# Splitting the second half of the key and query weights inside groups 0 and 1

## Chip, cores and metric

The kernel runs on one core of a Trainium2 chip. Its time is the device time of one execution in microseconds (us). The times before are 2044.08, 2043.05 and 2043.65 us, median 2043.65.

## What is computed

An input of 16 sequences of 512 tokens with 128 features goes through a layer norm; to the input are added an attention over the normed rows and a mixture of experts over them. All is in float32. Cut to what matters:

```python
xn = layernorm(x)
# attention: 16 heads of 64
h = rmsnorm(xn) * norm_scale
q, k, v = h @ wq, h @ wk, h @ wv          # each 128 x 1024
a = softmax((q * 64 ** -0.5) @ k.T) @ v   # per head
attn = a @ w_out + b_out
# experts: 8, the two best of each token
logits = silu(xn @ rw1 + rb1) @ rw2 + rb2
w, i = top_k(logits, 2); w = softmax(w)
ffn = sum(w_e * (silu(xn @ w1[e] + b1[e]) @ w2[e] + b2[e]))
out = x + attn + ffn
```

## The kernel before

Matrix products with the weights are done with each operand split into a high part (rounded to the faster float32r type) and a low part (the rest), as three matmuls into one PSUM bank (`three`, lines 237 to 240: low times high, high times low, high times high). The weights are split once. `split_weights` does this for chunks of 512 columns: ACT writes the high part (line 245), then either DVE (line 248) or POOL (line 252) subtracts it from the source and writes the low part. The raw weights are staged in parts of PT, a tile that later holds transposed probabilities.

Chunk 0 of WK and WQ serves head pairs 0 to 3 of a batch element, chunk 1 pairs 4 to 7. A pair of heads is worked on in two groups, so chunk 1 is first needed by the projections for pair 4.

The program is a list of operations for each engine, filled by `add` and emitted in order. Each operation has a name and the names that it needs, which become semaphore waits. Operations added between two calls of `q.close()` are sorted within an engine by their place: for DVE in a group with an even number the order is inverse, max0, max1, turn1, turn0, low, values, sums, side; in an odd one sums, max0, turn0, max1, turn1, values, inverse, low, side. For ACT it is turn0, exp00, exp01, high, exp10, exp11, values, side, hi, turn1 in an even group and turn0, exp00, values, exp01, high, turn1, exp10, side, exp11, hi in an odd one. What has no place goes to "side", in the order in which it was added. PE, POOL and SP keep the order of the program.

In front of the groups (the head of the program) stand: the statistics and normed rows of batch element 0, the split of chunk 0 of WK and WQ, the transposes into HT, the projections of pair 0 (`project`, whose result is split by ACT on line 378 and DVE on line 379), then a block of remaining splits (lines 866 to 870), the small operation RB1H (line 871, 4 columns on DVE), a memset of PM (872), and `turn_x(0)`, the transposes into XT with a cast on ACT (343) and the low part on DVE (344).

Then come groups 0 to 261, `group(G)`. On PE an even group runs scores S0, transposes T0, scores S1, T1, the next projection (kq), attending, experts and routing. Scores are line 394, row maxima of them DVE line 403, exponentials ACT line 409 with an accumulator read, transposes of probabilities PE line 424, copied out by ACT line 436 or DVE line 439. In group 0, `attending` adds four value tiles (lines 238 to 240 on PE; copied out by DVE on line 361 for the first, ACT on line 359 for the others), and `route` adds the first router matmuls (L238 to L240 with R), followed on ACT by TANH (line 555) and the copy HS (558), on POOL by lines 561 and 563. Reciprocals of the row sums are line 464. `starting(G)` is called inside the experts part of each group, before `route`, and adds what is to be done once at that group.

A planner (`take`, with fixed costs in `HOLD`) chooses PSUM banks while the program is written. The order of its choices isn't changed by operations that take no bank. Its choice for the third value tile of group 0 is the bank that held the key projection of pair 1, free once DVE has written that one's low part.

Of the kernel before, what the change touches and what calls it, by code (L numbers as in the profile page):

```python
# [20 lines left out]
DH = 64  # L21
# [44 lines left out]
class Queues:  # L66
# [7 lines left out]
    def add(self, engine, make, needs=(), name=None, step=1, sem=None, place="side"):  # L74
        key = None
        if name is not None:
            key = sem or (engine + "_" + name[0])
            self.count.setdefault(key, 0)
        self.open[engine].append((place, make, [n for n in needs if n is not None], name, key, step))
# [23 lines left out]
def block_kernel(nc, x, wq, wk, wv, wout, ns, bout, rw1, rb1, rw2, rb2, w1, w2, bias, ident, tri, consts, out):  # L103
# [11 lines left out]
    with ExitStack() as ctx:  # L115
        def sb(name, shape, dt=F32, to=ctx):
            return to.enter_context(nc.sbuf_tensor(name, shape, dt))
# [7 lines left out]
        WQ = sb("WQ", [P, 2, H * DH], F32R)  # L125
        WK = sb("WK", [P, 2, H * DH], F32R)
# [105 lines left out]
        wk_s = PT[:, 2, 0:2].rearrange("p a b -> p (a b)")  # L232
        wq_s = PT[:, 2, 2:4].rearrange("p a b -> p (a b)")
# [8 lines left out]
        def split_weights(name, src, dst, chunks, scale=1.0, on="pool"):  # L242
            for c in chunks:
                s = slice(c * 512, (c + 1) * 512)
                add("act", lambda e, s=s: e.mul(dst[:, 0, s], src[:, s], scale), needs=[("load", f"{name}{c}")],
                    name=("whi", name, c))
                if on == "dve":
                    add("dve", lambda e, s=s: e.scalar_tensor_tensor(dst[:, 1, s], src[:, s], scale, dst[:, 0, s],
                                                                     ALU.mult, ALU.subtract),
                        needs=[("whi", name, c)], name=("wlo", name, c))  # L250
                else:
                    add("pool", lambda e, s=s: e.tensor_tensor(dst[:, 1, s], src[:, s], dst[:, 0, s], ALU.subtract),
                        needs=[("whi", name, c)], name=("wlo", name, c))
# [610 lines left out]
            project(0, key)  # L864
        q.close()
        split_weights("wv", wv_s, WV, [0])
        split_weights("wk", wk_s, WK, [1], on="dve")
        split_weights("wv", wv_s, WV, [1])
        split_weights("wq", wq_s, WQ, [1], DH ** -0.5, on="dve")
        split_weights("r1", r1_s, R1, [0])  # L870
        add("dve", lambda e: e.tensor_scalar(RB1H[:], RB1[:], 0.5, None, ALU.mult), needs=[("load", "rb1")], name=("rb1h",))
        add("dve", lambda e: e.memset(PM[:, 0, 0], 0.0), name=("pm0",))
# [4 lines left out]
        turn_x(0)  # L877

        def starting(G):
            if G == 10:  # L880
                add("pool", lambda e: e.tensor_scalar(BIN[:, :, 8:16], BIN[:, :, 0:8], 0.5, None, ALU.mult),
                    needs=[("load", "bias")], name=("bhalf",))
            if G == 11:
                add("sp", lambda e: e.dma_start(b_tab.rearrange("e p c -> p e c"), BIN[:]), needs=[("bhalf",), ("load", "bias")],
                    name=("b_tab",), step=16, sem="b_tab")
            if G == 13:
                add("sp", lambda e: e.dma_start(out[T:T + S].rearrange("(t p) d -> p t d", p=P), PAD[:, :, 0:D]),
                    needs=[("pad0",)], name=("spare_out",), step=16, sem="spare_out")
            if 14 <= G < 14 + E - 1:
                k = G - 14  # L890
                add("sp", lambda e: e.dma_start(slots[E * REGION + k * S:E * REGION + (k + 1) * S]
                                                .rearrange("(t p) d -> p t d", p=P), PAD[:]),
                    needs=[("pad",)], name=("pads", "x", k), step=16, sem="pads")
            if G == 22:
                add("sp", lambda e: e.dma_start(out[EARLY * S:T], x[EARLY * S:T]), name=("base",), step=16, sem="base")
# [126 lines left out]
        def group(G):  # L1022
# [13 lines left out]
            for part in PE_ORDER[odd]:  # L1036
                if part in ("S0", "S1"):
                    score(int(part[1]))
                elif part in ("T0", "T1"):
                    if old:  # L1040
                        turn_probs(*old[int(part[1])])
                elif part == "kq":
                    if live and n + 1 < PAIRS:
                        project(n + 1, odd == 0)
                elif part == "inverse":
                    if even:
                        denominators(G // 2 - 1)
                elif part == "ahead":
                    halves_after(G)
                elif part == "attend":  # L1050
                    attending(G)
                elif part == "spread":
                    if even:
                        spread(G // 2 - 1)
                elif part == "route":
                    route(G)
                elif part == "experts":
                    starting(G)
                    splitting(G)
                    counting(G)  # L1060
                    experts(G)
                    again(G)
                elif part == "weighted":
                    if odd and 0 <= G - 3 < GROUPS:
                        weighted((G - 3) // 2)
# [76 lines left out]
```

How the kernel before makes its waits and increments, by code:

```python
    def emit(self, engine, eng, sems):  # L91
        seen = {}
        for make, needs, key, step in self.items[engine]:
            for sem, value in (self.value[n] for n in needs):
                if seen.get(sem, 0) < value:
                    eng.wait_ge(sems[sem], value)
                    seen[sem] = value
            ins = make(eng)
            if key is not None:
                ins.then_inc(sems[key], step)
# [974 lines left out]
        @block.sync  # L1075
        def _(eng):
            q.emit("sp", eng, sems)
            for k, v in q.count.items():
                if k.startswith(("st_", "sadd", "spare_out", "base", "rrow", "tab", "b_tab", "sc_", "pads")):
                    eng.wait_ge(sems[k], v)
```

## Time and profile before

| | |
|---|---|
| runs | 2044.08, 2043.05, 2043.65 us |
| profiled execution | 2040.24 us, span 2038.4 us |
| PE busy | 1947.9 us, 96% |
| ACT, DVE, POOL busy | 77%, 76%, 45% |
| mean granted TensorE clock | 0.99 |

A granted clock of 1.00 is 2.4 GHz and one of 0.50 is 1.2 GHz. Times of instructions are counted from the start of the span. Records of one engine may overlap by about 0.1 us, since an engine starts an instruction while the last one drains: the step from one start to the next is then less than the duration.

### The profile page before, as it was taken

The numbers are of one execution on the slowest core, as the hardware profiler recorded it, in microseconds if no ns is written. First come the engines' busy times: TensorE is split into PE (matmuls) and PEld (weight loads), VectorE is DVE, ScalarE is ACT, GpSimd is POOL, SyncE is SP. The second block draws the span as 40 slices with busy tenths as digits, with TensorE's granted clock in tenths as the row PEclk, the third lists the DMA queues.
The fourth block names the chain that finished last, engine by engine and source line by source line (L and its number), as shares of the span: only waits on it lengthen the run. The fifth ranks groups of instructions, "written<-read, shape, count | busy, mean of one in ns | idle before, by whom it ended". The sixth has DMA issues, their size and how long they took to land.

```text
span 2038.4 us, 45230 instructions
## 1 busy us (share of the span) xinstructions
PE 1947.9 (96%) x16646; PEld 1254.4 (62%) x16646; DVE 1539.4 (76%) x2654; ACT 1574.2 (77%) x3716; POOL 918.2 (45%) x790
## 2 busy tenths in 40 slices
PE   7999999999999999998889999999999999999997
PEld 5655555555656555564556666666666666666664
DVE  6878888887878777776767777777777777777774
ACT  5777777777777777775678888888888888888884
POOL 4344455453344444441014645546446455464454
PEclk9999999999999999999999999999999999999999
DMA  2023222221111111001313334344333343343332
GB/s 84 30 61 103 91 98 89 85 72 34 40 37 43 38 43 38 33 32 36 91 57 81 84 86 84 80 95 85 85 79 85 86 83 88 84 85 80 79 75 47
DMA packets 132697, 141.96 MB, mean 70 GB/s; under 512 B 25438, under 2 KB 99038, under 8 KB 132446
## 3 DMA queue, kind: packets, MB, share of 16 engines
q1 hardware_dynamic: 101886, 118.34, 18.4%
q0 software_dynamic: 30592, 20.73, 8.6%
q8 instruction: 134, 2.20, 0.5%
q14 instruction: 85, 0.70, 0.1%
HBM read 102.65 MB, written 38.46 MB: 69 GB/s over the span
## 4 chain that ended last, share of the span: by engine, by line
PE 75%; ACT 12%; DVE 6%; issue 4%; DMA 2%; another core or an unknown queue 1%; SPq 0%; POOL 0%; POOLq 0%; DVEq 0%; ACTq 0%
PE pair L453 21%; PE pair L394 15%; PE pair L424 10%; PE pair L238 6%; PE pair L240 5%; PE pair L239 4%; ACT PR L409 4%; PE pair L499 2%; PE pair L501 2%; DVE NM L403 2%; PE pair L787 1%; PE pair L788 1%; PE pair L786 1%; ACT PT L436 1%; ACT HS L558 1%
## 5 line engine op out<-in xcount | busy, mean ns | idle before, releaser
L409 ACT ACTIVATE PR<-pair,NM 128x512 f32<-128x512 f32 x1024 | 718.2, 722 | 21.3 <-DVE NM L403 18.8
L403 DVE TENSOR_REDUCE NM<-pair 128x2 f32<-128x1024 f32 x512 | 611.8, 1211 | 68.0 <-PE pair L394 47.9
L436 ACT COPY PT<-pair 128x512 f32<-128x512 f32 x640 | 358.2, 608 | 368.4 <-PE pair L424 364.4
L394 PE MATMUL pair<-KS,QS 64*128 64x512 f32 x3072 | 491.7, 424 | 20.5 <-DVE KS L379 12.3
L453 PE MATMUL pair<-PT,V 128*64 128x512 f32 x2048 | 471.0, 602 | 0.2
L424 PEld LDWEIGHTS pair<-idn,PR 64*128 64x128 f32 x8192 | 338.0, 139 | 100.8 <-ACT HS L558 27.0
L394 PEld LDWEIGHTS pair<-KS,QS 64*128 64x128 f32 x3072 | 257.8, 188 | 181.1 <-issue 126.2
L424 PE MATMUL pair<-idn,PR 64*128 64x64 f32 x8192 | 343.2, 223 | 21.0 <-ACT HS L558 15.9
L813 POOL DMA_INDIRECT out<-YS,IDW x156 | 246.9, 1583 | 187.2 <-DVE YS L805 128.6
L778 POOL TENSOR_TENSOR HH<-ZZ,HH 128x512 fp32r<-128x512 f32 x156 | 199.2, 1347 | 291.1 <-ACT HH L775 291.1
L453 PEld LDWEIGHTS pair<-PT,V 128*64 128x64 f32 x2048 | 136.4, 137 | 258.7 <-issue 252.5
L439 DVE COPY PT<-pair 128x512 f32<-128x512 f32 x384 | 250.8, 681 | 14.7 <-remote 9.6
L409 ACT ACTIVATION_READ_ACCUMULATOR PR<-pair,NM 128x1 f32 x1024 | 242.1, 236 | 0.0
L561 POOL TENSOR_TENSOR TH<-TH,HS 128x512 f32<-128x512 f32 x64 | 81.8, 1278 | 295.9 <-ACT HS L558 295.6
L459 DVE TENSOR_TENSOR OT<-pair,RB 128x512 f32<-128x512 f32 x128 | 88.4, 690 | 144.8 <-PE pair L453 136.2
L772 DVE SCALAR_TENSOR_TENSOR ZZ<-ZT,ZZ 128x512 f32<-128x512 f32 x156 | 110.5, 709 | 79.2 <-ACT ZZ L763 79.1
L664 POOL DMA_INDIRECT slots<-XR,IDX x128 | 125.8, 983 | 89.9 <-DVE junk L660 58.8
L379 DVE TENSOR_TENSOR QS<-pair,QS 128x512 fp32r<-128x512 f32 x128 | 88.5, 691 | 90.0 <-ACT QS L378 87.7
L761 ACT ACTIVATE ZT<-pair,BT 128x512 f32<-128x512 f32 x156 | 116.6, 747 | 1.5 <-PE pair L240 1.4
L763 ACT ACTIVATE ZZ<-pair,BT 128x512 f32<-128x512 f32 x156 | 117.7, 754 | 0.0
L379 DVE TENSOR_TENSOR KS<-pair,KS 128x512 fp32r<-128x512 f32 x128 | 87.3, 682 | 9.3 <-ACT KS L378 9.1
L378 ACT CAST QS<-pair 128x512 fp32r<-128x512 f32 x128 | 77.9, 609 | 15.6 <-PE pair L240 9.3
(168 smaller groups left out, 2807.9 us busy)
## 6 DMA issues: line engine op xcount, KB each, us to landing
E<-w_tab SPq DMA_DIRECT2D x78, 512.0 KB
RB<-l_rows SPq DMA_DIRECT2D x127, 256.0 KB
XG<-slots SPq DMA_DIRECT2D x39, 264.0 KB
w_tab<-SPL SPq DMA_DIRECT2D x16, 512.0 KB
l_rows<-RT SPq DMA_DIRECT2D x508, 1.0 KB
xin<-in_x SPq DMA_DIRECT2D x16, 256.0 KB
XQ<-in_x SPq DMA_DIRECT2D x16, 256.0 KB
RAW<-in_w SPq DMA_DIRECT2D x16, 256.0 KB
```

The costliest lines, as they stand in the source:

```text
L238: e.matmul(ps, w[1], m[0], start=True, stop=False)
L379: add("dve", lambda e: e.tensor_tensor(lo, bank[bk], hi, ALU.subtract), needs=[(name + "hi", n), *old], name=(name + "lo", n), place="low")
L394: m = e.matmul(bank[bk + j], a[half[j], cols], c[half[j], :], start=(k == 0), stop=(k == 2))
L403: add("dve", lambda e: e.tensor_reduce(NM[:, 2 * t:2 * t + 2], both[:], AX.X, ALU.max, negate=True), needs=[("S", n, t), *([("exp", n - 1, ...
L409: add("act", lambda e: e.activation(PR[:, k, :], bank[bk], ACT.Exp, bias=NM[:, k:k + 1], accum_out=RS[:, n % 2, j, t:t + 1]), needs=[("max ...
L424: m = e.transpose(bank[two[r]][:, at:at + DH], PR[rows, 2 * t + j, c * P:(c + 1) * P], idn[rows, rows])
L436: add("act", lambda e, r=r: e.copy(dst[r], src[r]), needs=[("T", n, t), *old], name=("PT", n, t, r), place=f"turn{t % 2}")
L439: add("dve", lambda e, r=r: e.tensor_copy(dst[r], src[r]), needs=[("T", n, t), *old], name=("PT", n, t, r), place=f"turn{t % 2}")
L453: m = e.matmul(bank[bk][j * DH:(j + 1) * DH, :], V[:, k, h * DH:(h + 1) * DH], PT[:, n % 2 * 2 + j, k, :], start=(k == 0), stop=(k == QT - 1))
L664: add("pool", lambda e, k=k, t=t: e.indirect_dma_start(slots, bass.IndirectOffsetOnAxis(ap=IDX[:, r % 2, k, t:t + 1], axis=0), XR[:, r % 2 ...
L778: add("pool", lambda e: e.tensor_tensor(lo, ZZ[:, r], hi, ALU.subtract), needs=[("hi", n), old], name=("lo", n))
L813: add("pool", lambda e, t=t: e.indirect_dma_start(out, bass.IndirectOffsetOnAxis(ap=IDW[:, i % 4, t, 0:1].bitcast(U32), axis=0), YS[:, i % ...
```

## The change

Two of the seven calls of `split_weights` are taken out of the head and done by `starting` in groups 0 and 1. Each is one operation on ACT and one on DVE, with 128 x 512 elements each. By the sorting rule they come to stand in "side": the one of WK behind the value copies of group 0 and in front of the router's TANH on ACT, and last in group 0 on DVE; the one of WQ between the last two exponentials of group 1 on ACT, and last in group 1 on DVE. No transfer is moved.

```diff
         split_weights("wv", wv_s, WV, [0])
-        split_weights("wk", wk_s, WK, [1], on="dve")
         split_weights("wv", wv_s, WV, [1])
-        split_weights("wq", wq_s, WQ, [1], DH ** -0.5, on="dve")
         split_weights("r1", r1_s, R1, [0])
...
         def starting(G):
+            if G == 0:
+                split_weights("wk", wk_s, WK, [1], on="dve")
+            if G == 1:
+                split_weights("wq", wq_s, WQ, [1], DH ** -0.5, on="dve")
             if G == 10:
```

## Rows read from the trace of the kernel before

**Rows 1.** The page: its span, and the busy time of each engine.

```profile
span 2038.4 us, 45230 instructions
...
PE 1947.9 (96%) x16646; PEld 1254.4 (62%) x16646; DVE 1539.4 (76%) x2654; ACT 1574.2 (77%) x3716; POOL 918.2 (45%) x790
```

**Rows 2.** Windows: us, busy PE, PEld, DVE, ACT, POOL, granted clock, DMA, GB/s.

```profile
17.30:21.30 4.00, 3.95 (x21) 2.66 (x21) 3.68 (x3) 2.33 (x5) 4.00 (x3) 1.00 0.00 0
21.30:26.30 5.00, 0.00 (x0) 0.00 (x0) 4.14 (x7) 2.67 (x8) 1.29 (x4) 0.99 0.00 0
26.30:30.20 3.90, 3.87 (x10) 3.12 (x11) 0.57 (x1) 2.24 (x5) 0.00 (x0) 0.57 0.00 0
...
36.20:40.00 3.80, 3.79 (x36) 3.07 (x38) 1.59 (x4) 2.51 (x7) 0.66 (x1) 0.55 0.01 1
```

**Rows 3.** Chain that ended last, in order of time: start us, us, what.

```profile
15.46 0.23 PE pair L239
...
17.07 0.53 ACT WK L245
...
17.62 1.37 DVE WK L248
19.00 1.70 DVE WQ L248
20.70 1.64 DVE RB1H L871
...
22.39 1.22 DVE NM L403
...
27.55 0.43 PE pair L240
```

**Rows 4.** Line 248: duration in ns, least/median/most, first and last start in us.

```profile
L248 DVE SCALAR_TENSOR_TENSOR WK<-PT,WK x2: 693/1033/1373, 7.0 to 17.6; 128x512 fp32r<-128x512 f32 x2
L248 DVE SCALAR_TENSOR_TENSOR WQ<-PT,WQ x2: 679/1228/1777, 11.8 to 18.9; 128x512 fp32r<-128x512 f32 x2
```

**Rows 5.** Timeline of DVE: start us, us, instruction, idle before and its releaser.

```profile
16.57 0.69 DVE L379 TENSOR_TENSOR QS<-pair,QS 128x512 fp32r<-128x512 f32 x1
...
21.79 0.67 DVE L344 TENSOR_TENSOR XT<-pair,XT 128x512 fp32r<-128x512 f32 x1
...
31.82 2.48 DVE L403 TENSOR_REDUCE NM<-pair 128x2 f32<-128x1024 f32 x2 [4.95 <-PE pair L394]
...
37.36 0.20 DVE L464 RECIPROCAL RI<-RS 128x8 f32<-128x8 f32 x1 [1.20 <-ACT PR L409]
...
37.73 1.20 DVE L403 TENSOR_REDUCE NM<-pair 128x2 f32<-128x1024 f32 x1
```

**Rows 6.** Timeline of ACT.

```profile
19.05 0.57 ACT L343 CAST XT<-pair 128x512 fp32r<-128x512 f32 x1
...
29.29 0.59 ACT L359 COPY V<-pair 128x512 f32<-128x512 f32 x1 [0.69 <-PE pair L240]
30.23 0.69 ACT L555 ACTIVATE TH<-pair,RB1H 128x512 f32<-128x512 f32 x1 [0.35 <-PE pair L240]
...
36.41 0.76 ACT L409 ACTIVATE PR<-pair,NM 128x512 f32<-128x512 f32 x1
...
38.56 1.07 ACT L436 COPY PT<-pair 128x512 f32<-128x512 f32 x2 [1.29 <-PE pair L424]
```

**Rows 7.** Timeline of POOL.

```profile
17.16 2.99 POOL L252 TENSOR_TENSOR WV<-PT,WV 128x512 fp32r<-128x512 f32 x2 [5.38 <-ACT WV L245]
20.11 1.73 POOL L252 TENSOR_TENSOR R<-PT,R 128x512 fp32r<-128x512 f32 x1
```

**Rows 8.** Timeline of PE, the restarts after standing still.

```profile
14.27 0.50 PE L238 MATMUL pair<-HT,WK 128*128 128x512 f32 x1 [1.63 <-DVE HT L329]
...
26.33 0.80 PE L238 MATMUL pair<-WV,HT 128*128 128x512 f32 x1 [5.05 <-DVE KS L379]
...
36.21 1.46 PE L394 MATMUL pair<-KS,QS 64*128 64x512 f32 x6 [1.79 <-DVE QS L379]
```

## Prediction

> **What bounds the kernel now.** I read the page first. PE is busy for 1947.9 us of a 2038.4 us span [rows 1], so most of the kernel is PE's, and a change that moves four small instructions can only be worth something where PE stands still. The second view is the table of windows over the first 40 us, because the four instructions stand there [rows 2]. From 17.3 to 21.3 us PE is busy 3.95 of 4.00 us; from 21.3 to 26.3 us it does nothing at all, while DVE is busy 4.14 us; from 26.3 to 30.2 us it is busy again, with ten matmuls in 3.87 us and a granted clock of 0.57 (a mixture of the two levels, 1.2 and 2.4 GHz, mostly the lower); from 36.2 to 40.0 us the clock is low again, 0.55.
>
> The third view is the chain of work that ended last, in order of time [rows 3]. The reader is to see that it walks through the very instructions of the change: the high half of WK's second chunk on ACT (0.53 us), then on DVE its low half (1.37 us), WQ's low half (1.70 us) and the small RB1H operation (1.64 us), and only then the first row maxima, at 22.39 us. Behind those maxima come the exponentials, the cast of the next key tile, its low half on DVE, and that last one frees PSUM bank 0, for which PE has waited 5.05 us when it starts the third value tile at 26.33 us [rows 8]. So the start of the program is one serial chain, and DVE's queue is its longest link. Nothing after it follows the clock on the wall: each later stage is released by instructions of the one before, and the four moved instructions take no PSUM bank, so the written order of all else stays as it is.
>
> **Step 1: what the removal in front of group 0 gives.** After the low half of Q (16.57 us, 0.69 long, to 17.26) DVE's queue will hold RB1H, then XT's low half, PM's memset, and the first maxima [rows 5]. Two things can hold it. XT's low half needs ACT's cast of XT, which began at 19.05 us [rows 6]; two ACT instructions of 0.53 us each [rows 3] leave the queue in front of it, so it begins at 19.05 - 1.06 = 17.99, ends 0.57 later at 18.56, and DVE can start on it at about 18.6. RB1H is the other. It has four columns, and took 1.64 us of the chain. The same low halves that took 0.69 and 0.68 us at the very start took 1.37 and 1.78 us here [rows 4], and what is different is that POOL runs its own subtractions, two in 2.99 us from 17.16 and a third of 1.73 us from 20.11 [rows 7]: XT's low half starts at 21.79, just as that third one ends (20.11 + 1.73 = 21.84). I read this as DVE and POOL taking turns. In the new order RB1H comes at 17.3, inside POOL's first subtraction, which ends half way through the 2.99 us, at about 18.65. That is the time at which XT's cast is ready too, so RB1H costs nothing beyond it. From XT's low half to the maxima it was 22.39 - 21.79 = 0.60 us. The maxima start at 18.6 + 0.6 = 19.2 in place of 22.39: **3.2 us** gained. The first scores are there in time: PE starts them when Q's low half is done at 17.3, and the 21 matmuls up to 21.3 are the 12 of the scores and nine dense ones behind them at 0.23 us [rows 2, 3], so the scores end at about 19.
> The bounds: if RB1H gets its turn only when POOL's second subtraction ends (17.16 + 2.99 = 20.15), the maxima start at 20.75 and 1.6 us are gained. More than 3.2 is excluded by XT's cast. The Trainium skill (GPSIMD Engine Reference, section 8, Key points) says that GpSimd shares its SBUF interfaces with VectorE and contends with instructions of two SBUF inputs or of a 2-port mode, and says nothing of turns: by it alone RB1H could be held for as long as POOL's subtractions follow each other, which would make step 1's term the 1.6 us or less and not the 3.2.
>
> **Step 2: PE's clock behind the stall.** The stall shrinks from 5.05 to 5.05 - 3.2 = 1.85 us. After the 5.05 us stall the clock was at the low level, and a dense matmul took a step of 0.43 us where it takes 0.23 at the high one [rows 3]. Is 1.85 us short enough to keep 2.4 GHz? The rows point both ways: before the first projection PE stood still for 1.63 us and the window behind shows no fall; before the scores at 36.21 it stood still for 1.79 us, and those six took 1.46 us at the low level [rows 8, 2]. What differs is the work around: in front of the second were transposes of 64 columns, in front of the first and of ours dense matmuls of 512. I take it that the clock holds, with the other case as a rival.
> Its worth is read at the next place where the chain is on ACT, the first TANH of the router at 30.23 us, 3.90 us after PE's restart [rows 6, 8]. At the high level the two value tiles take 0.4 us for the last matmul, 5 steps of 0.23 and some 0.1 for the first, 1.65 us; then ACT copies the last of them (one step of 0.53), does the moved high half of WK (0.53, see below) and reaches TANH 2.75 us after the restart, when PE's nine matmuls (2.35 us) are done as well. 3.90 - 2.75 = 1.15, and I take **1.2 us**. If the clock falls as before, this term is gone and turns into a cost of 0.1: the value copy starts 29.29, and two steps of 0.53 end at 30.35 in place of 30.23.
>
> **Step 3: what is added in group 0.** ACT's part is counted above. DVE's low half of WK (0.69 us alone; POOL has nothing to do at that time, its next work waits for the router) falls into the 4.95 us for which DVE waits in front of the next group's maxima [rows 5]: nothing. Without that cover it would be 0.7 us.
>
> **Step 4: what is added in group 1.** ACT's high half of WQ goes in front of the group's last exponential, which began at 36.41 us; behind it ACT waited 1.29 us for PE's transposes [rows 6], so 0.53 us are covered. DVE's low half of WQ (0.68 us) falls into the 1.20 us of waiting in front of the reciprocal; the reciprocal moves by 0.53 us, and the maxima behind it from 37.73 to about 38.2, ending 1.20 later at 39.4 [rows 5]. What needs them is an exponential that stands behind two copies on ACT which end at 38.56 + 1.07 = 39.63 and pass the engine on about 0.1 earlier [rows 6]. Covered, by a tenth of a us. If it isn't, or POOL doubles the operation to 1.78 us [rows 4], it costs 0.1 to 1.0 us. The queues of SP and POOL lose and get nothing: the first transposed probabilities that overwrite the staged weights are written at the earliest in group 3, two groups behind the last moved split, so their wait on it is met long before.
>
> **Sum.** 3.2 + 1.2 = 4.4 us, against the profiled execution's 2040.24 us (span 2038.4), which makes 2035.8. The median of the runs is 2043.65, 3.4 above that execution, and the change takes the same off it: 2043.65 - 4.4 = **2039.2 us**. 0.2% of the median is 4.1 us, about what a measurement of this kernel can tell from no change; the forecast lies just beyond it.
>
> **The rivals.**
> (a) The clock falls behind the short stall too. Rows 8 show it once after 1.79 us of standing still. Then the gain is 3.2 - 0.1 = 3.1: 2040.6 us. The Trainium skill (TensorE: Matmul & The Clock Gate, Part 1, What's actually happening) says that the clock's switching point isn't tied to the kernel's start and differs from run to run. No run here shows that; by it, several executions of one program would differ in this term, which the three times (1.0 us apart) neither show nor exclude. I give it 2 in 10.
> (b) RB1H waits for a second subtraction: the lower bound of step 1. Gain 1.6, with the clock's 1.2 at most 2.8: 2040.9 to 2042.0 us. Against it: between POOL's back-to-back subtractions WK's low half did get its turn (it ended at 18.99, 0.35 us after the first of them). 1 in 10.
> (c) The gain is given back later: the chain behind 40 us is bound elsewhere, or the moved instructions displace what is critical in group 1. Gain 0 to 1.5: 2042.2 to 2043.7. Against it: everything is released by this chain. 0.6 in 10.
> (d) Slower: PE's clock falls at other places. A fall costs about what it cost here, 1.2 us; the earlier start moves the work against the moments at which it switches, and later stages have stalls of PE of over a us too. It takes four more falls than now to use up 4.4 us, and eight to make the kernel slower by 0.2%; six would give 2043.65 - 4.4 + 7.2 = 2046.5 us. 0.4 in 10.
> (e) The forecast, 2039.2 us: 6 in 10. Its own range is 2038.3 to 2039.9: another 0.5 us if the second fall, at 36 us, goes away as well, 0.7 less if step 4's thin cover fails.
>
> **How the numbers follow.** The range reaches over the forecast, (a) and half of (b): 2038.3 to 2041.2, about 8 in 10. Faster by over 0.2% (below 2039.56) is three quarters of (e), with a little of the rest: 0.46. Slower by over 0.2% is the far part of (d): 0.03. The rest, 0.51, is within 0.2%, as a smaller gain, though the likeliest single time lies just outside.
>
> **What would show it.** In the profile after: the first row maxima at about 19.2 us, RB1H and XT's low half in front of them; PE's stall behind the second value tile about 1.9 us, with value matmuls of 0.4 us and not 0.63; the first TANH near 25.8 us; low halves of WK and WQ of about 0.7 us each, in DVE's waits near 26 and 32.7; PE's busy share unchanged. The prediction is wrong if the maxima start later than 20 us (step 1), if the granted clock behind the stall is 0.5 (step 2), or if the head shows the 4.4 us and the end doesn't.

## The result and the profile after

Over 17 runs of each, the changed kernel takes 2038.91 us (median) and the kernel before 2043.26 us. The ratio is 0.9979, with a 95% interval from 0.9972 to 0.9987: faster by 4.4 us, and by something between 2.7 and 5.7. The forecast was a gain of 4.4 us. (The three runs in front of the prediction had a median of 2043.65 us, the 17 one of 2043.26.)

The profiled execution of the changed kernel took 2040.83 us and that of before 2040.24, so these two executions show no gain at the end, although one is there at the head. Both halves of that have to be read.

The head first. Timeline of DVE in the changed kernel (start us, us, instruction, idle before), the counterpart of [rows 5] and [rows 3]:

```profile
15.82 0.69 DVE L379 TENSOR_TENSOR KS<-pair,KS 128x512 fp32r<-128x512 f32 x1 [1.68 <-ACT KS L378]
...
17.13 1.30 DVE L869 TENSOR_SCALAR RB1H<-RB 128x4 f32<-128x4 f32 x1
...
18.57 0.69 DVE L344 TENSOR_TENSOR XT<-pair,XT 128x512 fp32r<-128x512 f32 x1
19.18 2.35 DVE L403 TENSOR_REDUCE NM<-pair 128x2 f32<-128x1024 f32 x2
...
26.40 0.69 DVE L248 SCALAR_TENSOR_TENSOR WK<-PT,WK 128x512 fp32r<-128x512 f32 x1 [2.72 <-ACT WK L245]
...
33.79 0.69 DVE L248 SCALAR_TENSOR_TENSOR WQ<-PT,WQ 128x512 fp32r<-128x512 f32 x1 [1.00 <-ACT WQ L245]
```

The first row maxima start at 19.18 us in place of 22.39 [rows 3]. The moved low halves take 0.69 us each where they took 1.37 and 1.78 [rows 4], and stand in waits. RB1H waits for POOL's first subtraction and no longer sets anything: XT's low half follows ACT's cast.

PE's restart and the clock, timeline and windows of the changed kernel, the counterpart of [rows 8] and [rows 2]:

```profile
23.13 0.50 PE L238 MATMUL pair<-WV,HT 128*128 128x512 f32 x1 [1.93 <-DVE KS L379]
23.47 0.39 PE L239 MATMUL pair<-WV,HT 128*128 128x512 f32 x1
...
24.16 0.63 PE L239 MATMUL pair<-WV,HT 128*128 128x512 f32 x1
...
32.85 0.96 PE L394 MATMUL pair<-KS,QS 64*128 64x512 f32 x6 [1.59 <-DVE QS L379]
...
21.30:23.10 1.80, 0.00 (x0) 0.00 (x0) 0.94 (x3) 1.80 (x6) 0.36 (x3) 1.00 0.00 0
23.10:27.40 4.30, 4.27 (x12) 3.16 (x12) 1.27 (x2) 3.59 (x8) 0.00 (x0) 0.62 0.00 0
27.40:34.50 7.10, 5.31 (x70) 3.90 (x69) 4.43 (x5) 6.96 (x17) 5.08 (x4) 0.98 0.01 2
34.50:37.90 3.40, 3.33 (x24) 2.82 (x25) 3.16 (x5) 2.37 (x6) 0.00 (x0) 0.52 0.01 1
```

The stall is 1.93 us in place of 5.05. But the clock still fell: the matmuls are 0.39 us long at first and 0.63, the length at 1.2 GHz, from 24.1 us on. It fell again at 34.4 us. On ACT:

```profile
25.73 0.63 ACT L245 ACTIVATE WK<-PT 128x512 fp32r<-128x512 f32 x1
26.53 0.69 ACT L555 ACTIVATE TH<-pair,RB1H 128x512 f32<-128x512 f32 x1 [0.17 <-PE pair L240]
...
33.08 0.67 ACT L245 ACTIVATE WQ<-PT 128x512 fp32r<-128x512 f32 x1
33.60 0.73 ACT L409 ACTIVATE PR<-pair,NM 128x512 f32<-128x512 f32 x1
...
36.10 0.69 ACT L409 ACTIVATE PR<-pair,NM 128x512 f32<-128x512 f32 x1 [0.68 <-DVE NM L403]
```

The first TANH comes at 26.53 us in place of 30.23 [rows 6], 3.7 us earlier. PE's first scores of group 1, which follow at 27.66 us in place of 30.81, are only 3.15 us earlier. The last row is a wait that the kernel before does not have in this place, 0.68 us behind the row maxima of group 2, to which the split of WQ has made DVE late.

At the first attention output (line 459, pair 0) the changed kernel is 3.0 us ahead: 47.99 against 51.01. It is still 3.0 ahead at the seventh output, 131.16 against 134.13. At the 61st, 912.51 against 912.17, nothing is left of it. Whether the change or the execution took that back was the first question.

### The profile page after: what moved, and what is told of

Its sections match the earlier page's. It is cut to its first block, busy times and chain, and to the rows that moved or that the text cites. A ratio compares the mean times of both kernels' runs of the same rounds, so it can differ in the third digit from the quotient of the medians.

```text
span 2039.0 us, 45230 instructions
## 1 busy us (share of the span) xinstructions
PE 1950.4 (96%) x16646; PEld 1257.1 (62%) x16646; DVE 1538.8 (75%) x2654; ACT 1576.6 (77%) x3716; POOL 919.2 (45%) x790
## 4 chain that ended last, share of the span: by engine, by line
PE 75%; ACT 12%; DVE 6%; issue 3%; DMA 2%; another core or an unknown queue 1%; SPq 0%; POOL 0%; POOLq 0%; DVEq 0%; ACTq 0%
PE pair L453 21%; PE pair L394 15%; PE pair L424 10%; PE pair L238 6%; PE pair L240 5%; PE pair L239 4%; ACT PR L409 4%; DVE NM L403 2%; PE pair L499 2%; PE pair L501 2%; PE pair L787 1%; PE pair L788 1%; PE pair L786 1%; ACT PT L436 1%
## 5 line engine op out<-in xcount | busy, mean ns | idle before, releaser
L459 DVE TENSOR_TENSOR OT<-pair,RB 128x512 f32<-128x512 f32 x128 | 88.4, 691 | 145.8 <-PE pair L453 138.9
L378 ACT CAST KS<-pair 128x512 fp32r<-128x512 f32 x128 | 76.9, 601 | 17.6 <-PE pair L240 8.8
```

## The experiments

They ran on other chips than the pair above, and there the kernel before has a median of 1998.9 to 1999.7 us. The head as a whole lies up to 0.7 us earlier or later from one execution to the next, so places in it are counted from the start of the first low half of KS on DVE (15.88 us before, 15.82 after). The table holds the profiled execution of each kernel. "Falls" are the stretches at 1.2 GHz in the first 40 us. The last column is the time from the 7th to the 61st attention output.

| kernel | first maxima | TANH | first output L459 | falls | outputs 7 to 61 |
|---|---|---|---|---|---|
| before, first profile | 6.51 | 14.35 | 35.13 | 2 | 778.0 |
| after, first profile | 3.36 | 10.71 | 32.17 | 2 | 781.4 |
| before_again | 6.51 | 14.58 | 35.34 | 2 | 755.97 |
| after_again | 3.36 | 11.04 | 31.25 | 1 | 754.44 |
| wk_only | 4.83 | 11.77 | 32.15 | 1 | 751.84 |
| wq_only | 4.83 | 12.72 | 33.48 | 2 | 755.95 |
| rb1h_late | 5.93 | 13.07 | 33.27 | 2 | 752.06 |
| fill7 | 3.36 | 10.03 | 30.84 | 1 | 756.23 |
| fill16 | 6.51 | 12.86 | 32.55 | 0 | 752.16 |
| wq_g2 | 3.35 | 11.26 | 32.52 | 2 | 755.01 |
| later_xt | 2.46 | 9.70 | 31.01 | 1 | 752.14 |
| xt_g1 | 2.45 | 9.69 | 29.89 | 0 | 754.81 |
| xt_fill | 2.46 | 9.70 | 29.91 | 0 | 754.93 |

**The two kernels again.** No edit.

> The kernel before, unchanged, as a control: how much of the difference between two profiled executions is the execution's own. Theory (the later losses are the execution's own): its head is as in the first profile within 0.1 us (first row maxima at 22.4 us, first attention output of pair 0, line 459, at 51.0 us), and yet the time from that first output to the last output of line 459 differs from the first profile's 1974 us by a us or more. Rival (the change itself makes the body behind 50 us slower, by the 3 us that the head gained): that time agrees with the first profile's within 0.5 us.

> The changed kernel, as a control. Theory: first maxima at 19.2 us and first output of line 459 near 48.0 us (3.0 earlier than before) in every execution, or up to 1 us earlier when the clock does not fall behind the short stall; the stretch from the first to the last output of line 459 lies by chance on either side of the first profile's 1978 us, by a us or more, and the time is about 4 us less than before. Rival (the body is slower with the change): that stretch is again 3 to 4 us longer than that of the kernel before.

The kernel before against itself gave 1.0003 (0.9994 to 1.0011). The changed one gave 0.9979 (0.9970 to 0.9987), a median of 1994.59 against 1998.86 us, 4.3 us as in the first comparison. The places in the head repeat to a hundredth of a us (6.51 and 3.36) up to the first maxima. The stretch from the 7th to the 61st output is longer by 3.3 us with the change in the first pair of profiles and shorter by 1.5 us in the second. From the first output to the last, which the expectations name, it is 1974.3 and 1978.2 us in the first pair, 1936.7 and 1934.4 in the second. That speaks against the rival: the later loss is the executions' own.

What it consists of can be read too, and it is not the same in the two pairs. Over this stretch of the first pair, windows of PE (us, busy PE, granted clock, DMA share, GB/s) and DVE's waits (us in total, times, longest), before and after:

```profile
134.13:912.17 778.04, 745.72 (x6700) 1.00 0.18 58
DVE NM L403 <- remote: 10.6, 8, 2.2
DVE PT L439 <- remote: 4.4, 3, 1.7
...
131.16:912.51 781.35, 745.74 (x6700) 1.00 0.18 58
DVE NM L403 <- remote: 15.1, 9, 2.3
DVE PT L439 <- remote: 4.0, 3, 1.8
```

PE was busy for the same time in both, and the clock fell twice in both. What is longer is time without work: DVE waited 19.1 us in place of 15.0 for something that is none of the core's own engines ("remote"). The repeats, on another chip, have no such wait, with the change or without it. So nothing ties these waits to the change, though what they are for stays open.

On the other chips the stretch differs by the clock. Windows of PE alone, first of before_again:

```profile
250.00:262.00 12.00, 10.71 (x85) 0.86 0.19 76
...
308.00:320.00 12.00, 10.71 (x91) 0.86 0.18 65
...
420.00:432.00 12.00, 10.71 (x78) 0.86 0.17 67
432.00:889.00 457.00, 450.02 (x4094) 1.00 0.12 39
```

Then of wk_only:

```profile
130.00:300.00 170.00, 166.55 (x1535) 1.00 0.28 93
300.00:600.00 300.00, 293.10 (x2663) 1.00 0.19 62
600.00:882.00 282.00, 277.64 (x2507) 1.00 0.12 39
```

In the one the clock fell three times, in the other never, and the same 54 outputs took 755.97 and 751.84 us. Over all the profiles of these chips, the stretch is 751.8 to 752.2 us without a fall (four kernels), 754.4 to 755.0 with two (four), 755.95 to 756.2 with three (three): 1.3 to 1.4 us a fall between the means of these groups, whatever the kernel. The 1.5 us by which the repeat of the changed kernel is shorter is one fall less.

**Half of the change.** In wk_only just the split of WK is moved, in wq_only just that of WQ.

```diff
-        split_weights("wk", wk_s, WK, [1], on="dve")
...
+            if G == 0:
+                split_weights("wk", wk_s, WK, [1], on="dve")
```

> Only the split of WK's second half is moved (to group 0). Theory (DVE's queue, one subtraction at each of POOL's turns, is what holds the first maxima): WQ's low half takes the turn after POOL's first subtraction, RB1H the one after the second, and the maxima start at about 20.7 us, 1.6 earlier than before: half of the whole gain. Rival (ACT's queue is what counts): 0.5 us earlier, at 21.9.

> Only the split of WQ's second half is moved (to group 1). Theory: the same as with WK alone, maxima at about 20.7 us, 1.6 earlier than before, so that the two halves add up to the 3.2 of both. Rival (ACT's queue): 0.5 us earlier, 21.9. If the loss seen between the router's first TANH (3.7 us early) and the first attention output (3.0 early) comes from WQ's place in group 1, this kernel loses it too and the kernel with WK alone does not.

Timeline of DVE in wk_only:

```profile
17.80 0.85 DVE L248 SCALAR_TENSOR_TENSOR WQ<-PT,WQ 128x512 fp32r<-128x512 f32 x1 [0.88 <-ACT WQ L245]
18.57 1.25 DVE L870 TENSOR_SCALAR RB1H<-RB 128x4 f32<-128x4 f32 x1
19.76 0.67 DVE L344 TENSOR_TENSOR XT<-pair,XT 128x512 fp32r<-128x512 f32 x1
...
20.36 2.34 DVE L403 TENSOR_REDUCE NM<-pair 128x2 f32<-128x1024 f32 x2
```

Either half brings the first maxima 1.68 us forward (6.51 to 4.83), and both together 3.15: DVE's queue, not ACT's 0.5. The times are less even: 0.9981 (0.9972 to 0.9990) for WK alone, as good as both together, and 1.0000 (0.9992 to 1.0009) for WQ alone, although its first output came 1.65 to 1.86 us earlier. That is just beyond the 1.6 us that its interval allows. On the same chip WK alone has a median of 1994.64 us and the whole change 1994.59: that moving WQ's split adds anything at the end is not shown. From the TANH to the first output wq_only takes 20.76 us, as the kernel before does (20.78 and 20.76); the loss that the expectation asks about is taken up under wq_g2.

**RB1H alone.** The kernel before, with the line of RB1H moved into group 0.

```diff
-        add("dve", lambda e: e.tensor_scalar(RB1H[:], RB1[:], 0.5, None, ALU.mult), needs=[("load", "rb1")], name=("rb1h",))
...
+            if G == 0:
+                add("dve", lambda e: e.tensor_scalar(RB1H[:], RB1[:], 0.5, None, ALU.mult), needs=[("load", "rb1")], name=("rb1h",))
```

> The kernel before, with only the four-column operation RB1H moved from in front of the first group into group 0 (last on DVE). It took 1.64 us of the chain. Theory (it is cheap by itself and was only waiting for POOL's third subtraction): it lasts under 0.3 us in its new place, where POOL is idle, and the first row maxima start when WQ's low half is done and XT's is written, about 1.1 us earlier than before, counted from the first low half of KS (5.4 in place of 6.5 us). Rival (the operation itself takes 1.3 to 1.7 us, in each profile so far): it lasts as long in its new place, and the maxima are 1.6 us earlier.

```profile
20.15 1.77 DVE L248 SCALAR_TENSOR_TENSOR WQ<-PT,WQ 128x512 fp32r<-128x512 f32 x1
21.86 0.67 DVE L344 TENSOR_TENSOR XT<-pair,XT 128x512 fp32r<-128x512 f32 x1
...
22.46 2.34 DVE L403 TENSOR_REDUCE NM<-pair 128x2 f32<-128x1024 f32 x2
...
26.86 0.16 DVE L880 TENSOR_SCALAR RB1H<-RB 128x4 f32<-128x4 f32 x1
```

The same operation takes 0.16 us where POOL is idle, and took 1.24 to 1.72 beside POOL's subtractions. From the start of WQ's low half to the maxima it is 2.31 us in place of 22.39 - 18.92 = 3.47: 1.16 less, as expected. The place counted from KS, 5.93, missed the expected 5.4, since in this execution the low half of Q came 0.6 us late, before anything that was edited. The reason is the clock, which fell at 14.06 us, in the stall of 1.63 us in front of the first projection, where the kernel before stayed at 2.4 GHz [rows 8]. The projection then began with

```profile
14.23 0.79 PE L238 MATMUL pair<-HT,WK 128*128 128x512 f32 x1 [1.63 <-DVE HT L329]
```

The ratio is 0.9989 (0.9980 to 0.9998).

**The clock alone.** fill7 is the changed kernel with seven matmuls that do nothing but keep PE busy in its stall, fill16 the kernel before with sixteen.

```diff
                 for t in range(QT):
+                    if t == 2:
+                        for k in range(7):
+                            add("pe", lambda e: e.matmul(bank[3], WK[:, 0, 0:P], HT[:, 0, 0, :], start=True, stop=True),
+                                needs=[("xTs", 0, 1)])
                     values(0, 0, t)
```

> The changed kernel, with seven dense matmuls of 512 columns added in the 1.9 us for which PE stands still in group 0, written to a bank whose content is overwritten later. Theory (the clock fell at 24 us because of that stall): the clock stays at 2.4 GHz from 20 to 31 us, and the router's first TANH comes 0.7 us earlier than in the changed kernel (10.0 in place of 10.7 to 11.0 us after the first low half of KS). Rival (the fall is not tied to the stall): the granted clock is 0.5 for some us between 22 and 30 us as before.

> The kernel before, with sixteen dense matmuls of 512 columns added in its 5.1 us stall, written to a bank whose content is overwritten later. It measures the price of the clock's fall without the change. Theory (the fall costs the chain about 1.2 us up to the router's first TANH): the first row maxima stay 6.5 us behind the first low half of KS, the clock stays at 2.4 GHz behind the stall, and the TANH comes 13.1 us after the first low half of KS in place of 14.4 to 14.6. Rival (the price is less, as between the changed kernel and its filled one, 0.7 to 1.0): 13.6.

Timelines of PE and ACT in fill7:

```profile
20.91 1.79 PE L914 MATMUL pair<-HT,WK 128*128 128x512 f32 x7
23.00 0.50 PE L238 MATMUL pair<-WV,HT 128*128 128x512 f32 x1 [0.30 <-DVE KS L379]
...
24.27 0.39 PE L240 MATMUL pair<-WV,HT 128*128 128x512 f32 x1
...
25.72 0.68 ACT L555 ACTIVATE TH<-pair,RB1H 128x512 f32<-128x512 f32 x1
```

and windows of fill16, in the filled stall and behind it:

```profile
22.60:26.40 3.80, 3.80 (x17) 2.91 (x17) 2.94 (x4) 2.87 (x8) 0.00 (x0) 1.00 0.00 0
26.40:30.20 3.80, 3.80 (x27) 2.85 (x28) 0.38 (x1) 3.58 (x8) 0.15 (x1) 1.00 0.02 4
```

In both the clock stayed at 2.4 GHz behind the filled stall. Unfilled, a stall of 1.92 us or more in this place had a fall with it in all eight profiles, so it was the stall that let it fall. The Trainium skill (TensorE: Matmul & The Clock Gate, Part 1, What's actually happening) ties the clock to how busy PE has been; the traces agree, at 2.4 GHz with the fillers and 1.2 without. The TANH came 12.86 us after KS in the kernel before, which makes the fall there worth 1.5 to 1.7 us, and 10.03 in the changed one, where it is worth 0.7 to 1.0. At the same clock the change is then worth 12.86 - 10.03 = 2.83 us at this place, 0.3 less than the 3.15 of the maxima. WK's high half, which now stands in front of the TANH, is the likely reason; no run tests it.

The TANH is not where the chain goes on, though. PE's first scores of group 1 start 14.93 and 15.17 us after KS in the two profiles before, 13.42 in fill16, 11.84 in both profiles after and 10.28 in fill7. There the fall costs 1.5 and 1.75 us in the kernel before and 1.6 in the changed one, so about the same. The change is worth 3.1 us there without the fall and 3.1 and 3.3 with it, and the part by which the changed kernel was further ahead at the TANH is gone again.

The ratios are 0.9974 (0.9965 to 0.9983) for fill7 and 0.9990 (0.9980 to 1.0000) for fill16: whether the fillers help the whole kernel, these runs cannot tell.

**The place of WQ's split.** wq_g2 is the changed kernel with "G == 2" in place of "G == 1".

> The changed kernel, with the split of WQ's second half in group 2 in place of group 1. Theory (in group 1 it costs something: ACT's last exponential is half a us later and holds the scores of group 2, 0.26 us, and the reciprocal and maxima behind it, 0.68 us): those two waits are gone, and the first attention output comes 0.3 to 0.7 us earlier than in the changed kernel at the same clock. Rival (the place costs nothing, since the waits only take over from others): no difference over 0.1 us, or the same wait in group 2.

Timeline of ACT:

```profile
40.07 0.64 ACT L245 ACTIVATE WQ<-PT 128x512 fp32r<-128x512 f32 x1
40.59 0.69 ACT L555 ACTIVATE TH<-pair,RB1H 128x512 f32<-128x512 f32 x1
```

The waits in group 1 are gone, but in group 2 the high half stands in a row of ACT work without a gap, in front of the next TANH, and takes its 0.52 us there. From the first TANH to the first output it is 21.26 us with WQ in group 2, 21.46 in the first profile after, 20.78 before, each with the second fall. The expected gain did not come; 0.9987 (0.9977 to 0.9996). The rival holds: another wait took over.

What the place costs can be read over all thirteen profiles, from ACT's cast of Q in group 1 to the first TANH of group 2. From there to the first output it is 7.81 to 7.83 us in every one. The second fall is the one at 31 to 37 us.

| WQ's split | without the second fall | with it |
|---|---|---|
| in the head | 7.25 to 7.29 (wk_only, rb1h_late, fill16) | 8.37, 8.39 (before_again, before) |
| in group 1 | 7.79 to 7.82 (after_again, xt_g1, xt_fill) | 8.37, 8.43, 8.71 (wq_only, fill7, after) |
| in group 2 | none | 8.88, 8.93 (wq_g2, later_xt) |

In group 1 it costs 0.5 us where the second fall is missing, and 0 to 0.3 where it comes. In group 2 it costs 0.5 with the fall. The fall itself costs 1.1 us. One wait in this stretch is ACT's for the maxima of group 2, here of wk_only and after_again, both without the second fall:

```profile
36.71 0.69 ACT L409 ACTIVATE PR<-pair,NM 128x512 f32<-128x512 f32 x1 [0.17 <-DVE NM L403]
...
35.49 0.69 ACT L409 ACTIVATE PR<-pair,NM 128x512 f32<-128x512 f32 x1 [0.69 <-DVE NM L403]
```

**RB1H and XT's low half behind the maxima.** later_xt has both moved into group 0, behind the low half of the next key tile, with WQ in group 2; xt_g1 is the same with WQ in group 1.

```diff
-        add("dve", lambda e: e.tensor_scalar(RB1H[:], RB1[:], 0.5, None, ALU.mult), needs=[("load", "rb1")], name=("rb1h",))
...
             if G == 0:
+                later[0]()   # the low half of XT, place="low"
+                add("dve", lambda e: e.tensor_scalar(RB1H[:], RB1[:], 0.5, None, ALU.mult), needs=[("load", "rb1")], name=("rb1h",), place="low")
```

> The kernel with WQ's split in group 2, and RB1H and XT's low half on DVE also moved, behind the low half of the next key tile in group 0. Theory (DVE's queue is still the longest link of the head after the change): the first row maxima start when the first scores are done, 1.0 us earlier than in the changed kernel (2.3 in place of 3.36 us after the first low half of KS), and all behind is 1.0 us earlier. Rival (the head is by now bound by ACT or PE): under 0.3 us.

> The changed kernel, WQ's split in group 1 as the change has it, with RB1H and XT's low half moved behind the low half of the next key tile. Theory (this order is the better one, since in group 2 the split of WQ pushed the router's TANH back by half a us on ACT): maxima 2.4 us and TANH about 9.7 us after the first low half of KS, and the first attention output 0.3 to 0.5 us before that of the kernel with WQ in group 2; time 0.25 to 0.35% under the kernel before. Rival (the place of WQ makes no difference): the same as that kernel.

Timeline of DVE in later_xt:

```profile
17.80 2.36 DVE L411 TENSOR_REDUCE NM<-pair 128x2 f32<-128x1024 f32 x2 [1.06 <-PE pair L402]
21.01 0.69 DVE L387 TENSOR_TENSOR KS<-pair,KS 128x512 fp32r<-128x512 f32 x1 [0.86 <-ACT KS L386]
21.62 0.68 DVE L347 TENSOR_TENSOR XT<-pair,XT 128x512 fp32r<-128x512 f32 x1
22.22 0.16 DVE L887 TENSOR_SCALAR RB1H<-RB 128x4 f32<-128x4 f32 x1
```

DVE now waits for the first scores, so nothing is left to gain from its queue: the maxima are 0.9 us earlier than in the changed kernel, and PE's stall is down to 1.05 us, behind which no fall was seen. The ratios against the kernel before are 0.9970 (0.9958 to 0.9982) for later_xt and 0.9975 (0.9964 to 0.9987) for xt_g1, both with wide overlap with the change's 0.9979. So these heads are 0.9 us earlier, and no better time is shown. Between later_xt and xt_g1 the first output differs by 1.1 us, but one execution had the second fall and the other had none, and the fall alone is worth the 1.1 us.

**Filling the second stall.** xt_fill adds to xt_g1 five matmuls in front of the scores of group 2.

```diff
+                if G == 2 and t == 0:
+                    for k in range(5):
+                        add("pe", lambda e: e.matmul(bank[4], WK[:, 0, 0:P], HT[:, 0, 0, :], start=True, stop=True),
+                            needs=[("exp", 0, 2, 0), ("exp", 0, 2, 1)])
```

> The kernel of the run before this one, with five dense matmuls added while PE waits 1.6 to 1.8 us for the scores of group 2. Theory (the second fall of the clock, at 34 to 36 us, is due to that stall, and costs 0.5 to 1 us where it comes): the clock stays high over the first 50 us, and the first attention output is 0.5 to 0.9 us earlier than in the run before this one if that shows the fall, and the same if it doesn't. Rival: the clock falls there all the same.

Neither profile has a fall in the head, and the first outputs agree (29.89 and 29.91). That settles nothing on the second stall; the ratio is 0.9978 (0.9968 to 0.9989).

## Why the prediction was right, point by point

The forecast of 4.4 us was met by the two comparisons (4.4 and 4.3 us), and its sign and size are right. One of its two terms was not.

**Step 1** (3.2 us from DVE's queue) was right in all parts. The maxima started at 19.18 us (forecast 19.2), held by XT's cast; RB1H took its turn after POOL's first subtraction (it ended at 18.43 us, the subtraction at 18.41), and rb1h_late shows that it costs 0.16 us by itself. Either half of the change gives 1.68 us. Rival (b) is excluded.

**Step 2** is the step that failed, as the prediction put it: "I take it that the clock holds". It did not, in either profile of the changed kernel, and rival (a), with 2 chances in 10, described what happened to the clock. The prediction's reason for this was a misreading as well. It put dense matmuls in front of the stall that kept the clock and transposes in front of the one that did not. The last work of PE in front of each, in the timeline of the kernel before:

```profile
11.98 0.66 PE L321 MATMUL pair<-idn,HR 128*128 128x128 f32 x4 [1.12 <-DVE HR L291]
...
34.02 0.40 PE L240 MATMUL pair<-HT,WQ 128*128 128x512 f32 x1
```

It is the other way round: four transposes into HT before the first projection, and the last of three dense matmuls before the scores at 36.21 us. The price was also off, 1.2 us where fill16 shows 1.5 to 1.75. And since the clock fell in the changed kernel too, at the same price at PE's scores of group 1, the term came to nothing there: 3.15 us ahead, step 1 alone. At the TANH the changed kernel is further ahead (the fall costs 0.7 to 1.0 us up to there, since the first matmuls still run at 2.4 GHz), but its scores start 1.13 us behind the TANH where the kernel before has 0.58. The mechanism was right where its condition is met: with fillers the TANH comes at 10.03, against 14.35 before, a gain of 4.3 where 4.4 was worked out.

**Step 3** was right: WK's low half took 0.69 us in a wait of 2.72.

**Step 4** was mis-sized. It counted WQ's split in group 1 as covered, by a tenth of a us. By the table under wq_g2 it costs 0.5 us without the second fall, and 0, 0.1 and 0.3 with it. The cover was read from an execution in which the transposes of group 2 ran at the low clock (1.07 us). Where they run at 2.4 GHz, in 0.66 us, ACT's copies are done sooner, and ACT waits 0.7 us for the maxima that the split has made late, in place of 0.2.

**The sum at the head** is then 3.7 us at the TANH and 3.0 at the first output in the first pair of profiles, 3.5 and 4.1 in the second, where the changed kernel missed one fall. The prediction's 4.4 is above all four. The measured 4.4 has an interval from 2.7 to 5.7 and holds them all, and rival (a)'s 3.1 as well. So the change's own worth in the head is about 3.1 us, less up to 0.5 for WQ's place, and that the time came out at 4.4 to a tenth, with the 1.2 us of step 2 missing, was luck as far as these runs show. Where the last 0.3 to 1.4 us come from, fewer falls later or chance, these runs cannot tell. The lower end of the range, 2038.3, doesn't follow from its terms either: 4.4 and 0.5 for the second fall make 2038.75; the measured 2038.91 lies above both. Rival (c), that nothing arrives at the end, is what the first pair of profiles seemed to show, and the repeats refute it. Rival (d), more falls elsewhere, has its mechanism in the traces (1.3 to 1.4 us a fall), but not its sign.

## What to carry to other kernels

Work that nobody needs soon still costs its full time when it stands in the queue of the engine that the first link of the chain goes through, and here it cost twice its own time, because DVE and POOL took turns. Move it behind the first critical operation, into a wait that is there at either level of the clock: a cover read from one execution at the low clock may be gone at the high one. To judge a change of a few us, read the head in landmarks of two executions of each kernel, and take the time from many runs: one profile of each showed no gain where 17 runs did.

## What was not expected of the hardware

The granted clock fell behind a stall of 1.92 to 1.93 us between dense matmuls in all three profiles that have it, and not behind the 1.05 us of later_xt, xt_g1 and xt_fill. Behind the stall of 1.58 to 1.81 us in front of the scores of group 2 it fell in seven of twelve profiles (one kernel, after: at 34.4 us in the first profile, not in the second), and in the first stall of 1.63 us in one of thirteen. What decides between them no run here shows. A fall in the middle of the attention work costs 1.3 to 1.4 us.

The chip of the first pair was 2% slower (2043 against 1999 us), at the same mean clock of 0.99. The 54 outputs took 778 and 781 us there and 752 to 756 elsewhere. One difference is in the waits. DVE's remote ones shown above, 15.0 and 19.1 us over the 54 outputs, are absent on the other chips, and so are ACT's (3.7 and 4.0 us). Together they are most of the 23 and 27 us by which the stretch is longer than in the repeats of two falls; what they are waits for is left open.
